# One kernel of four transformer layers: the instruction orders of its last, six-deep layer laid out anew on every engine

## The reference

```python
for i in range(DEPTH):                                   # 6 layers
    x = attn_layer(shift_tokens(x), Wqkv[i], q_scale[i], k_scale[i], Wo[i]) + x
    x = ffn_layer(shift_tokens(x), ln_g[i], ln_b[i], W1[i], b1[i], W2[i], b2[i]) + x

def attn_layer(x, Wqkv, qs, ksc, Wo):
    qkv = x @ Wqkv                                       # 128 -> 3 x 16 heads x 64
    q, k = l2norm(q) * qs, l2norm(k) * ksc
    q = q * cos * scale + rotate_half(q) * sin * scale   # and k with 1 / scale
    out = local_attention(q, k, v)                       # windows of 32, each sees itself and the one before
    return out @ Wo

def ffn_layer(x, g, bln, W1, b1, W2, b2):
    xn = (x - mu) / jnp.sqrt(var + 1e-05) * g + bln
    a, gate = jnp.split(xn @ W1 + b1, 2, -1)             # 128 -> 2 x 341
    return a * gelu(gate) @ W2 + b2
```

## Time and profile before

| | |
|---|---|
| median of three runs | 3986.41 us (3983.93 to 3988.76) |
| the profiled execution | 3984.39 us, span 3982.6 us from the first to the last instruction |
| mean granted clock of PE | 0.972 |
| PE busy | 3698.1 us (93%) |
| DVE, POOL, ACT busy | 2933.1 (74%), 2734.3 (69%), 2368.4 us (59%) |

### The profile page before, as it was taken

How to read it: one execution, slowest core, us unless ns; L and a number is a source line. 1 busy time by engine, 2 the same in 40 slices (tenths; PEclk the granted TensorE clock), 3 DMA queues, 4 the chain that set the end, 5 groups by cost and what they waited for, 6 DMA issues and landing times.

```text
span 3982.6 us, 149155 instructions
## 1 busy us (share of the span) xinstructions
PE 3698.1 (93%) x64720; PEld 2771.7 (70%) x64720; DVE 2933.1 (74%) x5190; ACT 2368.4 (59%) x4275; POOL 2734.3 (69%) x3122
## 2 busy tenths in 40 slices
PE   6889899869999899998999989999899998999996
PEld 3444444337888778887888877888778887788774
DVE  3566665558888778887788877888778887888762
ACT  3222221126777677776777766777667776777663
POOL 0222222259988788887888878888788887888771
PEclk9999999879999999999999999999999999999998
DMA  1000000011111111121211111111111111111110
GB/s 70 3 6 6 6 3 3 13 38 48 43 39 44 46 47 45 36 48 42 52 37 43 42 46 48 39 41 47 43 48 40 42 45 45 44 41 47 38 40 22
DMA packets 96269, 146.97 MB, mean 37 GB/s; under 512 B 27264, under 2 KB 35840, under 8 KB 95488
## 3 DMA queue, kind: packets, MB, share of 16 engines
q1 hardware_dynamic: 95616, 137.42, 13.8%
HBM read 32.46 MB, written 4.19 MB: 9 GB/s over the span
## 4 chain that ended last, share of the span: by engine, by line
PE 87%; DVE 4%; issue 3%; ACT 2%; POOL 2%; DMA 1%; SPq 0%; ACTq 0%; POOLq 0%; DVEq 0%
PE bank L452 22%; PE bank L524 10%; PE bank L535 9%; PE bank L497 7%; PE bank L385 6%; PE bank L462 5%; PE bank L472 4%; PE bank L508 4%; PE bank L598 3%; PE bank L576 3%; PE bank L587 3%; PE bank L400 2%; PE bank L484 2%; PE bank L427 1%; PE bank L432 1%
## 5 line engine op out<-in xcount | busy, mean ns | idle before, releaser
L452 PE MATMUL bank<-wqkv,xs 128*128 128x512 f32 x3456 | 1068.0, 425 | 19.6 <-DVE m L847 15.3
L1380 POOL TENSOR_TENSOR m<-m 128x512 f32<-128x512 f32 x576 | 729.3, 1287 | 29.6 <-DVE m L847 27.1
L452 PEld LDWEIGHTS bank<-wqkv,xs 128*128 128x128 f32 x3456 | 586.3, 192 | 147.6 <-issue 61.5
L1134 ACT ACTIVATE sq<-bank 128x512 f32<-128x512 f32 x768 | 459.2, 598 | 113.1 <-PE bank L452 68.4
L847 DVE TENSOR_TENSOR m<-bank,tab 128x512 f32<-128x512 f32 x768 | 523.0, 681 | 0.9 <-POOL m L1380 0.8
L858 DVE TENSOR_REDUCE ss<-sq 128x8 f32<-128x512 f32 x768 | 506.1, 676 | 0.0
L1388 POOL TENSOR_TENSOR S<-S,nw 128x1024 f32<-128x1024 f32 x192 | 383.4, 1997 | 162.7 <-DVE S L878 162.7
L1396 POOL TENSOR_TENSOR S<-S,rs 128x512 f32<-128x512 f32 x384 | 411.4, 1092 | 62.2 <-DVE rs L892 61.0
L845 DVE TENSOR_TENSOR m<-bank,tab 128x512 f32<-128x512 f32 x576 | 393.3, 683 | 64.2 <-ACT sq L1134 47.2
L524 PEld LDWEIGHTS bank<-P,big 64*64 64x64 f32 x24576 | 378.6, 135 | 83.3 <-issue 75.3
L524 PE MATMUL bank<-P,big 64*64 64x32 f32 x24576 | 401.3, 220 | 6.5 <-issue 5.6
(11 more groups left out here) (211 smaller groups left out, 6997.0 us busy)
## 6 DMA issues: line engine op xcount, KB each, us to landing
big<-vst SPq DMA_DIRECT2D x1536, 64.0 KB, 2.0
stage<-in_wqkv SPq DMA_DIRECT2D x36, 256.0 KB, 3.0
tab<-in_tab SPq DMA_DIRECT2D x48, 128.0 KB, 2.3
big<-in_wa SPq DMA_DIRECT2D x1, 3460.0 KB, 12.1
wo<-in_wo SPq DMA_DIRECT2D x6, 512.0 KB, 3.6
big<-in_x SPq DMA_DIRECT2D x8, 256.0 KB, 3.0
keep<-Xr SPq DMA_DIRECT2D x8, 256.0 KB, 2.0
stage<-keep SPq DMA_DIRECT2D x8, 256.0 KB, 3.0
```

The costliest lines, as they stand in the source:

```text
L452: m = eng.matmul(pb[:, :], xt[a], wqkv[:, z, 512 * part:512 * part + 512], start=(n == 0), stop=(n == 2))
L1134: eng.activation(sq[:, part % 2, :], bank[part % 2][:, :], ACT.Square, scale=1.0, bias=0.0).then_inc(s["a_sq"], 1)
L1380: eng.tensor_tensor(turned(g, part), turned(g, part), m2[:, part % 2, :], ALU.add).then_inc(s["g_add"], 1)
```

## The change

The same calls with the same arguments in another order, in the loop of PE, DVE, ACT and POOL; SP's loop stays. The loop of each engine is also cut at another place: some calls that stood at the end of pass n stand at the head of pass n + 1, with the index moved along (`proj(n, 5)` became `proj(n - 1, 5)`, `chain(n)` became `chain(n - 1)`). `TURN` follows the new order of the projections, `centre` goes from bank 3 to bank 2, and `variance` and `down` go from bank 2 to bank 3. No instruction is added or taken away.

```diff
@@ -24,10 +24,10 @@
 MAGIC = 1597463007.0
 NU = DEPTH * NC
 NG = 4 * NU
-TURN = (0, 1, 4, 2, 3, 5)
+TURN = (0, 1, 2, 4, 3, 5)
 RING = {"tk": (3, 2), "tq": (3, 2), "pr": (3, 2), "v": (2, 3), "wo": 3,
-        "centre": 3, "variance": 2, "spread": 2, "gate": (2, 3, 2), "up": (2, 3, 3),
-        "down": 2}
+        "centre": 2, "variance": 3, "spread": 2, "gate": (2, 3, 2), "up": (2, 3, 3),
+        "down": 3}
 STEPS, ROUNDS = 12, NG + 20
 MAGIC2, FIRST = 1595932665.0, 0.703952253
 ROOT = 1.0
@@ -632,43 +632,42 @@
 
             for n in range(NG + 26):
                 q4, u = n % 4, n // 4
+                proj(n - 1, 5)
+                if q4 == 2:
+                    gate(u - 4, 2)
+                sim(n - 3)
+                turn_q(n - 1, 0)
+                turn_q(n - 1, 1)
                 proj(n, 0)
                 probs(n - 4, 0)
                 proj(n, 1)
                 probs(n - 4, 1)
                 out_proj(n - 5)
-                if q4 == 3:
-                    down(u - 4)
                 if q4 == 2:
                     up(u - 4, 0)
                     up(u - 4, 1)
                 if q4 == 1:
                     gate(u - 4, 0)
-                    gate(u - 4, 1)
                 if q4 == 3:
                     centre(u - 2)
                     end_centre(u - 5)
-                values(n - 4)
-                proj(n, 4)
-                if q4 == 2:
-                    up(u - 4, 2)
+                    down(u - 4)
                 proj(n, 2)
                 if q4 == 2:
                     spread(u - 3)
                     end_spread(u - 6)
+                    up(u - 4, 2)
+                if q4 == 1:
+                    gate(u - 4, 1)
+                values(n - 4)
+                if q4 == 3:
+                    variance(u - 2)
+                    end_variance(u - 5)
+                proj(n, 4)
                 turn_k(n - 2, 0)
                 proj(n, 3)
                 turn_k(n - 2, 1)
                 mask(n - 2)
-                proj(n, 5)
-                if q4 == 3:
-                    variance(u - 2)
-                    end_variance(u - 5)
-                if q4 == 1:
-                    gate(u - 4, 2)
-                sim(n - 2)
-                turn_q(n, 0)
-                turn_q(n, 1)
 
         @block.vector
         def _(eng):
@@ -977,40 +976,38 @@
             low(0)
             for n in range(NG + 26):
                 q4, u = n % 4, n // 4
+                rotate(n - 1, 2)
+                weights(n - 1, 2)
+                if q4 == 2:
+                    low(u + 1)
                 reduced(n - 1, 3)
+                rotate(n - 1, 3)
+                weights(n - 1, 3)
+                weights(n - 1, 4)
+                weights(n - 1, 5)
                 largest(n - 3)
                 lessened(n - 3)
-                if q4 == 3:
-                    low(u + 1)
                 rotate(n, 0)
                 weights(n, 0)
                 reduced(n, 0)
                 residual(n - 5)
-                reduced(n, 1)
+                if q4 == 3:
+                    xn_low(u - 3)
                 if q4 == 2:
                     hidden(u - 4, 0)
+                    hidden(u - 4, 1)
+                reduced(n, 1)
                 rotate(n, 1)
                 weights(n, 1)
                 if q4 == 2:
-                    hidden(u - 4, 1)
+                    normed(u - 3)
+                    ended(u - 6)
+                    hidden(u - 4, 2)
+                summed(n - 3)
                 if q4 == 3:
                     closed(u - 4)
-                summed(n - 3)
-                if q4 == 2:
-                    hidden(u - 4, 2)
+                reduced(n, 2)
                 inverted(n - 3)
-                if q4 == 3:
-                    xn_low(u - 3)
-                if q4 == 2:
-                    normed(u - 3)
-                    ended(u - 6)
-                rotate(n, 2)
-                weights(n, 2)
-                weights(n, 3)
-                rotate(n, 3)
-                weights(n, 4)
-                weights(n, 5)
-                reduced(n, 2)
                 if q4 == 3:
                     norm_step(u - 2)
                     end_step(u - 5)
@@ -1265,9 +1262,25 @@
             high(0)
             for n in range(NG + 26):
                 q4, u = n % 4, n // 4
-                out_turned(n - 5, 1)
+                if q4 == 2:
+                    gelu(u - 4, 0)
+                    gelu(u - 4, 1)
+                square(n - 1, 2)
+                if q4 == 3:
+                    scaled(u - 3)
+                v_out(n - 1, 0)
+                turned_k(n - 3, 0)
+                turned_k(n - 3, 1)
+                square(n - 1, 3)
+                v_out(n - 1, 1)
+                weights(n - 1, 2)
+                weights(n - 1, 3)
+                weights(n - 1, 4)
+                weights(n - 1, 5)
+                out_turned(n - 5, 0)
                 if q4 == 2:
                     gelu(u - 4, 2)
+                out_turned(n - 5, 1)
                 turned_q(n - 1, 0)
                 turned_q(n - 1, 1)
                 square(n, 0)
@@ -1276,33 +1289,16 @@
                 square(n, 1)
                 weights(n, 1)
                 probs(n - 4, 1)
-                if q4 == 2:
-                    shifted(u - 2)
                 if q4 == 3:
-                    scaled(u - 3)
+                    xn_high(u - 3)
                 if q4 == 0:
                     high(u + 1)
-                exps(n - 3)
                 if q4 == 1:
-                    gelu(u - 4, 0)
-                if q4 == 3:
-                    xn_high(u - 3)
-                if q4 == 1:
-                    gelu(u - 4, 1)
+                    shifted(u - 2)
                 if q4 == 3:
                     centred(u - 2)
                     end_centred(u - 5)
-                v_out(n, 0)
-                square(n, 2)
-                turned_k(n - 2, 0)
-                square(n, 3)
-                turned_k(n - 2, 1)
-                out_turned(n - 4, 0)
-                v_out(n, 1)
-                weights(n, 2)
-                weights(n, 3)
-                weights(n, 4)
-                weights(n, 5)
+                exps(n - 3)
 
         @block.gpsimd
         def _(eng):
@@ -1406,18 +1402,18 @@
             tables(0)
             for n in range(NG + 26):
                 q4, u = n % 4, n // 4
+                add(n - 1, 2)
+                if q4 == 2:
+                    tables(u + 1)
+                chain(n - 1)
                 weighed(n - 3)
+                add(n - 1, 3)
                 scale(n - 2, 0)
                 scale(n - 2, 1)
                 add(n, 0)
                 add(n, 1)
                 divide(n - 3, 0)
                 divide(n - 3, 1)
-                if q4 == 3:
-                    tables(u + 1)
-                add(n, 2)
-                add(n, 3)
-                chain(n)
 
 
 def shape_constants():
```

## The result

The changed kernel takes 4030.38 us (median of 4 runs, 4025.49 to 4034.49) against 3987.39 us of the kernel before on the same chip: ratio 1.0109, 95% interval 1.0091 to 1.0126. The forecast was 3987 us, 3970 to 4006.

What follows compares the result with a forecast made beforehand. PE's own order and durations were taken to bound the kernel; -4 + 2 + 7 - 4 + 0 = +1 us on the profiled 3984.39 us gave 3985.4, 3987 as the median. Its 8-in-10 range was 3970 to 4006.

Steps and rivals of the forecast that it cites:

- PE's stream (-4): PE's order in the steady units: longer runs save nothing, one toll before `sim` may go; -4 us (-4 to 0).
- tolls: Time PE loses at a change of matmul shape; 0.10 us a unit was to go at `sim` over some 43 units.
- Banks (+2): Bank handovers to PE in steady units all fit, three by 0.1 to 0.4 us; +2 us for small stalls (0 to +13).
- the dearer table switch: Rival: ACT's table load carries a drain as long, PE stands 0.8 us in 43 units, 4021 us; chance 0.03.
- Changes of layer (+7): Five layer changes: PE's stop moves behind ACT's first query tile copy, last weight copy later; +7 us (-5 to +15).
- Drain (-4): Last units: `end_centre` starts first, so ACT's copy runs under `down`; -4 us (-8 to 0).
- start (0): Kernel start: first rotation waits for the tables, first key tiles for the same POOL chain; 0 us (2 either way).
- one-bank rival: Rival: PE stands in every unit for one thin bank handover, 0.3 us a unit, 3998 us; chance 0.2.
- rival of the changes of layer: Rival: the longer stop at layer changes costs 3 us more each, 3995 to 4002 us; chance 0.09.
- R: Experiments' theory, not the prediction's: a wait holding PE's sequencer delays its next 256 instructions, so `sim`'s back half comes late.

Runs made afterwards that it cites:

- projection 4's move: Projection 4 ahead of `values` in the first group: kernel before 3976.45 us; changed kernel with VectorE's third and fourth weight subtraction adjacent 4005.78 us.
- p4_first_before: The kernel before with projection 4 ahead of `values` in the first group of each unit alone: 3976.45 us, ratio 0.9976.
- extra_wait: The late wait: kernel before, with TensorE also waiting ahead of the second `turn_k` for ScalarE's square of part 2: 3997.34 us, ratio 1.0023.
- extra_wait_early: Control: kernel before with one more TensorE wait ahead of the second `turn_k`, for ScalarE's earlier square of part 1: 3990.96 us, ratio 1.0003.

## Why the prediction was wrong

**PE's stream (-4): the step that failed.** It said "PE is in order, so only neighbours count" and "longer runs save nothing: 0". PE's order also sets how far ahead of the dense blocks the last wait is released, and in the first group the back half of `sim` comes late when that is less than about 3 us. Moving projection 2 ahead of `values` brought v_out from 2.78 to 2.09 us ahead of `sim` in the first group, and in the fourth, where the variance moved too, from 3.56 to 2.08. `sim` takes 0.26 us more in the first group and 0.09 to 0.10 in the third and fourth: +20.1 us in all, the largest term, where the prediction had 0. The late wait and projection 4's move show this for the first group. The third group is no case of it: its last release came 1.98 us ahead of `sim` before and 2.09 in the changed kernel. The earlier trace rows is one line of a list that also has waits marked issue, and the prediction leaves them out. In `values` the same kind of gap came to +7.0, mostly in the third and fourth group; which release delays those packets I did not trace.

In the same step, tolls. "Old and new order both have one stretch into and one out of `values`" holds in number but not in price: ahead of `values` up 2 takes 0.87 us (0.70 before), while up 1, which stood there, gives back only 0.09: +0.09 us in each unit, 4 us. And the variance's 0.10 us gain did not come: comparing medians of the fourth group, the variance takes 0.04 us more, the projection that is now next to `sim` 0.09, projection 4 0.02 less. About +0.1 a unit, so +4 to +5 where I had -4. These three are read off the block times; no run isolates them.

**Banks (+2).** Right: no handover of the steady state shows a wait, GELU and `scale` come in time, and the dearer table switch (a rival at 4021) did not appear: in the changed kernel `exps` ends at 2626.59 and the first GELU starts at 2627.91, 1.32 us later, with the load of 1.28 us between them. That is less than the 2.66 us for load and drain of the Trainium skill, "ScalarE: Activation LUTs", section "What ACT_TABLE_LOAD costs". But "does PE wait" was the wrong question for `turn_k`: v_out ends 0.35 us ahead of its transposes (2491.99, 2492.34), which is free for PE and not for its sequencer.

**Changes of layer (+7).** +7.8 measured in the sums of the two profiled runs, at the place and by the mechanism forecast; undoing the split of the subtractions took 8.2 away.

**Drain (-4), start (0).** +3.0 behind proj(191,0), which is within the scatter of this stretch, so these runs neither show the -4 nor refute it: 141.4, 145.3 and 151.7 us in p4_first_before, extra_wait and extra_wait_early, whose drain is that of the kernel before. The copy does run under `down`, but `end_variance` now claims `down`'s bank and waits for VectorE to empty it, which I overlooked. From the chain of the changed kernel:

```profile
3993.18 2.59 PE bank L598 x6
3995.79 0.76 DVE Xr L954
3996.69 1.02 PE bank L618 x8
```

0.90 us from VectorE's start to L618, where the earlier trace rows had 1.18.

**Rivals.** The one-bank rival (3998) did not happen, and its 0.3 us a unit is too small as well: the steady groups lost 43.4 us, 1.0 us a unit. The rival of the changes of layer (3 us more each) did not happen either. No rival had the instruction supply.

**Open.** `sim`s whose page edge is in the front half take 1.27 us from first to last matmul in the first and third group before and 1.36 to 1.40 in the changed kernel, from small gaps at the middle of `sim`. This goes with projection 4's move (1.27 again) and is not brought by the late wait (1.27), so it isn't explained by R as stated; it is some 0.1 us in two groups a unit, up to 9 of the 20 us, and nearly all that the third group lost. The +10.0 us of the projections and their neighbours are explained only as far as the tolls above. What the new orders of DVE, ACT and POOL cost by themselves stays open but for the change of layer: the one other order of TensorE that they were run with adds three waits a unit.

## What to carry to other kernels

Where a block issues hundreds of short instructions, look at how long before it the last semaphore wait of TensorE is released, not only whether TensorE stands at it. Keep eviction-bound waits away from dense blocks: here the same projection, one place earlier, gave 0.24% in one kernel and 0.56% in the other. Read the waits marked issue in the trace before saying that a reordering of an engine costs nothing. A hybrid of two complete schedules measured its own new waits here; a single added wait, with its control, measured the mechanism.

## What the runs showed of the hardware

TensorE gets its instructions in packets of 256 (16 KB: 512 packets for 131,061 instructions), nine in ten of which took 0.9 to 1.5 us here. Where one came late for a `sim` of the changed kernel (40 cases outside the changes of layer), it started 0.9 to 1.9 us after the last semaphore wait of the sequencer had ended, 1.1 in the median, and the first instruction of its page started 1.2 to 1.6 us after its end. From release to instruction that is 3.3 to 4.5 us, about three times the length of a 256-instruction `sim`. A wait that TensorE itself never stands at cost 0.2 us in one group of four (1.75 us for 1.53), because of that.
